# Up units of 256, 256 and 128 slots in one PSUM bank each, four units deep

## The chip, the cores and the metric

One core of one Trainium2 chip runs the kernel. The metric is the device time of one execution in microseconds; smaller is better. Engines: PE multiplies matrices (PEld is its weight loading), DVE and ACT work elementwise, POOL issues the indirect DMAs here, SP the plain ones.

## The reference, cut to what matters

A layer norm and a selective scan come first; the change does not touch them. Then comes a mixture of experts over T = 2048 tokens of width 128, with 8 experts of hidden width 512, the two best experts per token and 640 slots per expert:

```python
pre = jnp.einsum('ech,edh->ecd', expert_inputs, ff_pre_act_weight)
gate = jnp.einsum('ech,edh->ecd', expert_inputs, gate_weight)
expert_out = jnp.einsum('ecd,ehd->ech', pre * jax.nn.silu(gate), ff_post_act_weight)
updates = eo_flat[dispatch] * kept_w.astype(x.dtype)[:, None]
out = jnp.zeros((T, DMODEL), x.dtype).at[st].add(updates)
```

`expert_inputs` is 8 x 640 x 128, the rows of the tokens chosen for each expert.

## The kernel before

Everything is float32. The expert stage begins at about 204 us of a span of 352 us. Experts 0 to 7 are worked off one after another, each over 640 slots (`CAP`), as five tiles of 128 slots (`NQ` = 5) on the slot side and four chunks of 128 on the hidden side (`FC` = 4). The queues of all engines are written out by hand and meet in semaphores. For expert e:

- POOL (`gather`, L1213) fetches the 640 rows with five indirect DMAs, by the index list `gid` that DVE writes (L804), and later adds the 640 results to `out` with five more (L1230). Its order is: gathers of expert e + 2, then scatters of expert e. Ahead of the first scatter of an expert it waits until all earlier scatters have landed (`s_scattered`). Experts 6 and 7 have no gathers ahead of their scatters.
- PE turns the rows (`turn`, L1506) for the next expert; ACT and DVE split them into a high and a low f32r part (L1056, L1058, L821).
- `up` (L1517): a *unit* is one chunk of 128 hidden rows by one half of the slots (`HALF` = 320). A unit needs the gate product and the value product, each of them three f32r matmuls of 128x128 weights by 320 columns (`three`, L1510: high by high, high by low, low by high). There are 8 units, so 48 matmuls. The gate goes to PSUM bank 2 or 3, the value to bank 0 or 1, by the unit's parity. PE may start the gate of unit g when the silu of unit g - 2 has read its bank (`s_silu`), and its value when DVE has multiplied unit g - 2 (`s_hidden`).
- ACT (`gates`, L1060) applies silu to a unit's gate (L1067) into one of two `sg` buffers, and between the first five units scales one tile of the previous expert's result each (`weigh`, L1083), which that expert's scatter waits for. In the last two units it also copies the next expert's up weights (L1050).
- DVE (`expert`, L830) first computes the scatter ids and weights of the expert (`scatter_rows`, L812 to L815), for which it waits until the scatters of expert e - 2 have landed. Then for each unit it multiplies value by silu into `hT` (L841) and builds two of the 16 one-hot blocks of expert e + 2 (L787). Then come `columns`, `tokens_low`, `weights_low`, and `gather_rows(e + 2)`, which turns the table into `gid`.
- PE then runs `down` (L1537, 40 matmul instructions, two per f32 product) in three parts, with `turn` for expert e + 1 after the first part and `table(e + 2)` (L1491) ahead of the last. `table(e + 2)` needs the one-hots, and `gid` of expert e + 2 needs the table.
- SP (L422 to L426) reloads the weight buffers when `s_in_low` and `s_down` say that they are free.

So the path from one expert to POOL's next burst of gathers is: scatters of e - 2 landed, DVE `scatter_rows(e)`, first product, PE's remaining up units, part of `down` and `turn`, `table(e + 2)`, `gid`, gathers of e + 2.

`last_expert` (L1559) interleaves the up units of expert 7 with its down tiles, which go to PSUM banks of their own. `keep_clock` runs matmuls on zeros ahead of the stage.

Of the kernel before, what the change touches and what calls it, by code (L numbers as in the profile page):

```python
# [27 lines left out]
ALU = mybir.AluOpType  # L28
# [6 lines left out]
NT = T // P  # L35
# [23 lines left out]
HALF = CAP // 2  # L59
# [45 lines left out]
def build(nc, x, wx, wdt, vectors, dskip, w1, wg, w2, consts, jbits, out, rows):  # L105
    with ExitStack() as ctx:
# [116 lines left out]
        sg = later(2, HALF)  # L223
# [209 lines left out]
        def _(dve):  # L433
# [396 lines left out]
            def expert(e, b, more, split=True, last=False):  # L830
# [4 lines left out]
                for un in range(2 * FC):  # L835
                    half, f = un // FC, un % FC
                    dve.wait_ge(s_silu, e * (2 * FC) + (un + 1))
                    if un == 0:
                        if above_zero(e - 1):
                            dve.wait_ge(s_down, e - 1)  # L840
                    v.tensor_tensor(hT[:, b, f, half * HALF:(half + 1) * HALF], psum[:, un % 2, 0:HALF],  # L841
                                    sg[:, un % 2, :], ALU.mult).then_inc(s_hidden, 1)
                    if more:
                        for j in range(un * NT // (2 * FC), (un + 1) * NT // (2 * FC)):
                            one_hot(e + 2, j)
# [40 lines left out]
        def _(act):  # L886
# [165 lines left out]
            def spread_tokens(e, b):  # L1052
                if above_zero((e - 1) * 2 * FC):
                    act.wait_ge(s_up, (e - 1) * 2 * FC)
# [5 lines left out]
            def gates(e, b, i, split, first=False, last=False):  # L1060

                for un in range(2 * FC):
                    g = e * (2 * FC) + un
                    act.wait_ge(s_up, g + 1)
                    if above_zero(g - 1):
                        act.wait_ge(s_hidden, g - 1)
                    a.activation(sg[:, un % 2, :], psum[:, 2 + un % 2, 0:HALF], ACT.Silu).then_inc(s_silu, 1)  # L1067
                    if not first and un < NQ:
                        weigh(e - 1, 1 - b, un)
                    if last and un == 2 * FC - 2:  # L1070
                        weigh_last(e, b, range(2))
                    if split and un >= 2 * FC - 2:
                        if un == 2 * FC - 2:
                            act.wait_ge(s_in_weights[1 - b], 32 * (i + b) + 32)
                        weights_high(e + 1, 1 - b, un - 2 * FC + 2)
# [174 lines left out]
        def _(pe):  # L1250
# [266 lines left out]
            def up(e, b, units):  # L1517
                if 0 in units:
                    pe.wait_ge(s_in_low, 2 * e + 2)
                for un in units:  # L1520
                    half, f = un // FC, un % FC
                    g = e * (2 * FC) + un
                    pe.wait_ge(s_xe_low, 2 * e + 1 + half)
                    if above_zero(g - 1):
                        pe.wait_ge(s_silu, g - 1)
                    cs = slice(half * HALF, (half + 1) * HALF)
                    three(psum[:, 2 + un % 2, 0:HALF], f, b, 0, cs)
                    if above_zero(g - 1):
                        pe.wait_ge(s_hidden, g - 1)
# [89 lines left out]
```

## Time and profile before

| | us |
|---|---|
| median of 3 runs | 355.86 |
| lowest and highest | 352.87, 357.71 |
| the profiled execution | 354.3 |
| its span | 352.3 |
| PE busy (share of span) | 272.9 (77%) |
| DVE busy | 255.8 (73%) |
| POOL busy | 216.3 (61%) |
| PE weight loads busy | 195.2 (55%) |
| ACT busy | 131.8 (37%) |

The shares are means over the whole span; in the first half DVE's scan sets the pace, in the expert stage the shares are others. The rows shown further down are from the stage from 204 us on, apart from one. In a timeline row the first number is the start in us from the span's start, the second the length of the instruction, or of the merged run of equal ones. Matmuls overlap, so the length of one is more than the distance to the next; the distance from one start to the next (the pitch) is the rate. "[0.30 <-issue]" means that the engine was idle 0.30 us before, and what ended that.

### The profile page before, as it was taken

The page shows a single profiled execution, that of the slowest core. Times are in us where ns is not written, and L with a number is a line of the kernel's source. Part 1 is how long each engine was busy: PE and PEld are TensorE (multiplying, and loading weights), DVE is VectorE, ACT ScalarE, POOL GpSimd, SP SyncE. Part 2 cuts the span into 40 slices and gives each one's busy share as a digit, 9 for nine tenths or more (in the row PEclk, how much of TensorE's full clock was granted, in tenths as well). Part 3 has the DMA queues.
Part 4 walks back from the last instruction along what each step waited for, and adds up shares of the span by engine and source line. Part 5 has one row for each costly group of instructions (what it writes and reads, how often), then busy time and mean ns, then how long its engine had stood idle before and what let it go on. Part 6 is the DMA issues. An engine that isn't in the chain of part 4 may idle for free.

```text
span 352.3 us, 5061 instructions
## 1 busy us (share of the span) xinstructions
PE 272.9 (77%) x1432; PEld 195.2 (55%) x1432; DVE 255.8 (73%) x599; ACT 131.8 (37%) x270; POOL 216.3 (61%) x152
## 2 busy tenths in 40 slices
PE   5979997589688959866970868995979798978830
PEld 3345443145354425433460557994979798878730
DVE  2788599999999999999988855683757576533400
ACT  3374793415254244433102004361535244434410
POOL 2555637698656747565715055178888787876863
PEclk9895899769899989998995799999898989989995
DMA  7013004239200000000011012056253535423322
GB/s 217 0 40 82 0 4 116 60 84 243 100 31 0 0 30 30 0 30 30 0 55 64 3 32 46 7 130 130 43 134 40 134 33 136 63 47 37 33 22 22
DMA packets 20755, 20.30 MB, mean 58 GB/s; under 512 B 2624, under 2 KB 14848, under 8 KB 20736
## 3 DMA queue, kind: packets, MB, share of 16 engines
q1 hardware_dynamic: 13184, 14.63, 14.7%
q0 software_dynamic: 7040, 5.25, 11.5%
q10 hardware_dynamic: 512, 0.19, 0.3%
q8 instruction: 9, 0.15, 0.2%
q14 instruction: 10, 0.08, 0.1%
HBM read 10.82 MB, written 5.05 MB: 45 GB/s over the span
## 4 chain that ended last, share of the span: by engine, by line
DVE 25%; issue 21%; PE 20%; POOL 18%; DMA 9%; ACT 4%; POOLq 1%; DVEq 1%; ACTq 0%
POOL out L1230 10%; DMA out<-ring,sid 7%; DVE psum L525 6%; DVE ring L535 5%; POOL ring L1158 4%; PE psum L1513 3%; PE psum L1515 2%; PE psum L1514 2%; PE psum L1326 1%; PE psum L1298 1%; POOL parts L1143 1%; PE psum L1364 1%; PE psum L1534 1%; DMA small<-in_small 1%; DVE sm L558 1%
## 5 line engine op out<-in xcount | busy, mean ns | idle before, releaser
L1158 POOL TENSOR_TENSOR ring<-ring,cbc 128x1024 f32<-128x1024 f32 x31 | 73.2, 2363 | 44.6 <-DVE ring L535 44.2
L1230 POOL DMA_INDIRECT out<-ring,sid x40 | 64.0, 1601 | 16.8 <-issue 10.7
L1326 PE MATMUL psum<-stack,sel_r 128*128 (+1 forms) x120 | 51.6, 526 | 24.5 <-DVE ring L535 22.5
L1364 PE MATMUL psum<-ring,cst 128*128 128x512 f32 x128 | 67.2, 654 | 0.9 <-POOL ring L1158 0.9
L1213 POOL DMA_INDIRECT ring<-rows,gid x40 | 38.9, 971 | 36.4 <-issue 23.3
L535 DVE TENSOR_TENSOR_SCAN ring<-ring,psum 128x1024 f32<-128x1024 f32 x25 | 57.1, 2285 | 1.6
L1513 PE MATMUL psum<-stack 128*128 128x320 f32 x128 | 43.9, 343 | 15.0 <-DVE ring L841 14.4
L962 ACT ACTIVATE ring<-psum,nega 128x510 f32<-128x510 f32 x64 | 40.6, 681 | 38.2 <-PE psum L1326 35.4
L1326 PEld LDWEIGHTS psum<-stack,sel_r 128*128 128x128 f32 x120 | 22.1, 201 | 51.9 <-DVE ring L535 24.2
L1067 ACT ACTIVATE ring<-psum 128x320 f32<-128x320 f32 x64 | 27.9, 438 | 61.0 <-PE psum L1515 60.6
L841 DVE TENSOR_TENSOR ring<-psum,ring 128x320 f32<-128x320 f32 x64 | 31.2, 491 | 18.9 <-ACT ring L1067 17.6
L1515 PE MATMUL psum<-stack 128*128 128x320 f32 x128 | 42.3, 331 | 0.0
L1514 PE MATMUL psum<-stack 128*128 128x320 f32 x128 | 42.3, 330 | 0.0
L1534 PE MATMUL psum<-w_s,ring 128*128 128x128 f32 x320 | 40.0, 277 | 1.1 <-DVE ring L841 1.1
L1364 PEld LDWEIGHTS psum<-ring,cst 128*128 128x128 f32 x128 | 25.9, 209 | 24.1 <-issue 20.2
L1534 PEld LDWEIGHTS psum<-w_s,ring 128*128 128x128 f32 x320 | 37.7, 192 | 1.5 <-DVE ring L841 1.3
L1513 PEld LDWEIGHTS psum<-stack 128*128 128x128 f32 x128 | 26.6, 207 | 17.0 <-DVE ring L841 16.0
L525 DVE TENSOR_TENSOR psum<-psum,bbc 128x512 f32<-128x512 f32 x50 | 31.7, 680 | 0.0
L1298 PE MATMUL psum<-zero 128*128 128x256 bf16 x182 | 26.3, 307 | 6.0 <-DMA cst<-in_consts 3.5
L1298 PEld LDWEIGHTS psum<-zero 128*128 128x128 bf16 x182 | 19.6, 110 | 12.6 <-issue 5.2
L787 DVE TENSOR_SCALAR ring<-iota_b,r 128x128 bf16<-128x128 bf16 x128 | 26.5, 269 | 0.0
L1514 PEld LDWEIGHTS psum<-stack 128*128 128x128 f32 x128 | 26.5, 207 | 0.0
(181 smaller groups left out, 352.8 us busy)
## 6 DMA issues: line engine op xcount, KB each, us to landing
stack<-parts SPq DMA_DIRECT2D x16, 256.0 KB, 3.8
win_s<-in_wg SPq DMA_DIRECT2D x8, 256.0 KB, 3.6
win_s<-in_w SPq DMA_DIRECT2D x8, 256.0 KB, 4.3
w_s<-in_w SPq DMA_DIRECT2D x8, 256.0 KB, 2.9
xt<-in_x SPq DMA_DIRECT2D x4, 256.0 KB, 4.5
out<-xt SPq DMA_DIRECT2D x4, 256.0 KB, 2.3
rows<-xn SPq DMA_DIRECT2D x4, 256.0 KB, 2.3
ring<-rows,gid POOLq DMA_INDIRECT x40, 3.1
```

The source lines that it names most:

```text
L525: v.tensor_tensor(dst, src, bbc[:, bass.ts(c, CH)], ALU.mult).then_inc(s_input, 1)
L535: v.tensor_tensor_scan(hh[:, s].rearrange("p a b -> p (a b)"), da[:, s].rearrange("p a b -> p (a b)"), inputs.rearrange("p a b -> p (a b)" ...
L962: a.activation(dst[:, :, 1:], src[:, :, 1:], ACT.Exp, scale=nega[:, g:g + 1]).then_inc(s_decay, 1)
L1158: g.tensor_tensor(hc[:, s], hh[:, s], cb, ALU.mult).then_inc(s_product, 1)
L1230: g.indirect_dma_start(out=out, out_offset=bass.IndirectOffsetOnAxis(ap=sid[:, b, q:q + 1], axis=0), in_=ye[:, b, q, :], in_offset=None, c ...
L1298: mm(bank(junk, 2 * D), z[:, 0:P], z, start=True, stop=True)
L1326: ins = mm(bank(to), sel, stack[:, half, kind, bass.ts(c, CH)], start=True, stop=True)
L1364: ins = mm(bank(YB), wred[:, o:o + D], hc[:, s, k, :], start=(grp == 0), stop=(grp == NG - 1))
L1513: mm(out_, win_p[:, b, 0, k, fs], xe_p[:, b, 0, cs], start=True, stop=False)
L1514: mm(out_, win_p[:, b, 0, k, fs], xe_p[:, b, 1, cs], start=False, stop=False)
L1515: return mm(out_, win_p[:, b, 1, k, fs], xe_p[:, b, 0, cs], start=False, stop=True)
L1534: ins = mm(place, hT[:, b, f, q * P:(q + 1) * P], w2_s[:, b, f, :], start=(f == 0), stop=(f == FC - 1))
```

## The change

The slots of a chunk are cut in pieces of 256, 256 and 128 (`PIECES`) in place of two halves of 320, so an expert has `UNITS` = 12 units in place of 8. A unit's gate takes columns 0 to 255 and its value columns 256 to 511 of one PSUM bank, and four banks and four `sg` buffers are used in turn (`DEPTH` = 4). Both products of unit g now wait for one thing, the product of unit g - 4 on DVE (`s_hidden`). The silu of a unit waits for the same. The one-hots of an expert are spread over 12 units. The down tiles wait for the pieces that they read. The weight copies of ACT stay in the last two units of an expert. `weigh` stays in the first five.

```diff
--- before.py
+++ after.py
@@ -56,7 +56,10 @@
 CAP = 640
 NQ = CAP // P
 QA = 3
-HALF = CAP // 2
+
+PIECES = ((0, 256), (256, 512), (512, CAP))
+UNITS = len(PIECES) * FC
+DEPTH = 4
 EPS_LN = 1e-05
 EPS_W = 1.1920929e-07
 NROUND = 8
@@ -220,7 +223,7 @@
         stack_flat = stack[:].rearrange("p h k t -> p (h k t)")
         win_p = stack_flat[:, 0:8 * DFF].rearrange("p (b i k f) -> p b i k f", b=2, i=2, k=2)
         xe_p = stack_flat[:, 8 * DFF:8 * DFF + 4 * CAP].rearrange("p (b i n) -> p b i n", b=2, i=2)
-        sg = later(2, HALF)
+        sg = later(DEPTH, 256)
         hT = later(2, FC, CAP)
         ye = later(2, NQ, D)
         zero = sb("zero", [P, D])
@@ -832,16 +835,16 @@
                 scatter_rows(e, b)
                 if more:
                     dve.wait_ge(s_table, e + 2)
-                for un in range(2 * FC):
-                    half, f = un // FC, un % FC
-                    dve.wait_ge(s_silu, e * (2 * FC) + (un + 1))
+                for un in range(UNITS):
+                    (lo, hi), f = PIECES[un // FC], un % FC
+                    dve.wait_ge(s_silu, e * UNITS + (un + 1))
                     if un == 0:
                         if above_zero(e - 1):
                             dve.wait_ge(s_down, e - 1)
-                    v.tensor_tensor(hT[:, b, f, half * HALF:(half + 1) * HALF], psum[:, un % 2, 0:HALF],
-                                    sg[:, un % 2, :], ALU.mult).then_inc(s_hidden, 1)
+                    v.tensor_tensor(hT[:, b, f, lo:hi], psum[:, un % DEPTH, 256:256 + hi - lo],
+                                    sg[:, un % DEPTH, 0:hi - lo], ALU.mult).then_inc(s_hidden, 1)
                     if more:
-                        for j in range(un * NT // (2 * FC), (un + 1) * NT // (2 * FC)):
+                        for j in range(un * NT // UNITS, (un + 1) * NT // UNITS):
                             one_hot(e + 2, j)
                 if more:
                     columns(e + 2)
@@ -1050,8 +1053,8 @@
                 a.activation(win_p[:, b, 0, k], win_s[:, b, k], ACT.Copy).then_inc(s_in_high, 1)
 
             def spread_tokens(e, b):
-                if above_zero((e - 1) * 2 * FC):
-                    act.wait_ge(s_up, (e - 1) * 2 * FC)
+                if above_zero((e - 1) * UNITS):
+                    act.wait_ge(s_up, (e - 1) * UNITS)
                 act.wait_ge(s_rows_turned, 2 * e + 1)
                 a.activation(xe_p[:, b, 0, 0:QA * P], bank(4, QA * P), ACT.Copy).then_inc(s_xe, 1)
                 act.wait_ge(s_rows_turned, 2 * e + 2)
@@ -1059,20 +1062,21 @@
 
             def gates(e, b, i, split, first=False, last=False):
 
-                for un in range(2 * FC):
-                    g = e * (2 * FC) + un
+                for un in range(UNITS):
+                    lo, hi = PIECES[un // FC]
+                    g = e * UNITS + un
                     act.wait_ge(s_up, g + 1)
-                    if above_zero(g - 1):
-                        act.wait_ge(s_hidden, g - 1)
-                    a.activation(sg[:, un % 2, :], psum[:, 2 + un % 2, 0:HALF], ACT.Silu).then_inc(s_silu, 1)
+                    if above_zero(g - (DEPTH - 1)):
+                        act.wait_ge(s_hidden, g - (DEPTH - 1))
+                    a.activation(sg[:, un % DEPTH, 0:hi - lo], psum[:, un % DEPTH, 0:hi - lo], ACT.Silu).then_inc(s_silu, 1)
                     if not first and un < NQ:
                         weigh(e - 1, 1 - b, un)
-                    if last and un == 2 * FC - 2:
+                    if last and un == UNITS - 2:
                         weigh_last(e, b, range(2))
-                    if split and un >= 2 * FC - 2:
-                        if un == 2 * FC - 2:
+                    if split and un >= UNITS - 2:
+                        if un == UNITS - 2:
                             act.wait_ge(s_in_weights[1 - b], 32 * (i + b) + 32)
-                        weights_high(e + 1, 1 - b, un - 2 * FC + 2)
+                        weights_high(e + 1, 1 - b, un - UNITS + 2)
 
             def weigh(e, b, q):
                 if q == 0:
@@ -1518,16 +1522,13 @@
                 if 0 in units:
                     pe.wait_ge(s_in_low, 2 * e + 2)
                 for un in units:
-                    half, f = un // FC, un % FC
-                    g = e * (2 * FC) + un
-                    pe.wait_ge(s_xe_low, 2 * e + 1 + half)
-                    if above_zero(g - 1):
-                        pe.wait_ge(s_silu, g - 1)
-                    cs = slice(half * HALF, (half + 1) * HALF)
-                    three(psum[:, 2 + un % 2, 0:HALF], f, b, 0, cs)
-                    if above_zero(g - 1):
-                        pe.wait_ge(s_hidden, g - 1)
-                    three(psum[:, un % 2, 0:HALF], f, b, 1, cs).then_inc(s_up, 1)
+                    (lo, hi), f = PIECES[un // FC], un % FC
+                    g = e * UNITS + un
+                    pe.wait_ge(s_xe_low, 2 * e + 1 + (un >= FC))
+                    if above_zero(g - (DEPTH - 1)):
+                        pe.wait_ge(s_hidden, g - (DEPTH - 1))
+                    three(psum[:, un % DEPTH, 0:hi - lo], f, b, 0, slice(lo, hi))
+                    three(psum[:, un % DEPTH, 256:256 + hi - lo], f, b, 1, slice(lo, hi)).then_inc(s_up, 1)
 
             def down_tile(b, q, place):
                 for f in range(FC):
@@ -1540,14 +1541,14 @@
                     if above_zero(NQ * e):
                         pe.wait_ge(s_weighed, NQ * e)
 
-                pe.wait_ge(s_hidden, e * 2 * FC + (FC if tiles[-1] < 2 else 2 * FC))
+                pe.wait_ge(s_hidden, e * UNITS + FC * (tiles[-1] // 2 + 1))
                 for q in tiles:
                     ins = down_tile(b, q, psum[:, 5 + q // 4, (q % 4) * P:(q % 4 + 1) * P])
                 return ins
 
             def expert(i, b, more=True):
                 e = 2 * i + b
-                up(e, b, range(2 * FC))
+                up(e, b, range(UNITS))
                 down(e, b, i, range(0, 2))
                 turn(e + 1, 1 - b, i + b)
                 down(e, b, i, range(2, 4))
@@ -1561,12 +1562,12 @@
                 up(e, b, range(FC + 2))
                 pe.wait_ge(s_out_weights[b], 16 * (E // 2))
                 pe.wait_ge(s_weighed, NQ * e)
-                pe.wait_ge(s_hidden, e * 2 * FC + FC)
+                pe.wait_ge(s_hidden, e * UNITS + FC)
                 for q in range(2):
                     down_tile(b, q, bank(LAST_BANK[q], P)).then_inc(s_down_tile, 1)
-                up(e, b, range(FC + 2, 2 * FC))
-                pe.wait_ge(s_hidden, (e + 1) * 2 * FC)
+                up(e, b, range(FC + 2, UNITS))
                 for q in range(2, NQ):
+                    pe.wait_ge(s_hidden, e * UNITS + FC * (q // 2 + 1))
                     down_tile(b, q, bank(LAST_BANK[q], P)).then_inc(s_down_tile, 1)
 
             keep_clock(WARM["slots"], 3)
```

## Rows read from the trace of the kernel before

**Rows 1.** Windows of all engines: stretch, length, busy us (count) per engine, PEclk.

```profile
213.90:221.70 7.80, 7.25 (x49) 6.93 (x48) 5.81 (x24) 4.63 (x9) 2.66 (x3) 1.00 0.17 35
...
227.80:323.70 95.90, 83.14 (x645) 81.64 (x644) 57.31 (x197) 39.38 (x103) 77.52 (x60) 0.93 0.45 85
```

**Rows 2.** Timeline, POOL: start us, us taken, instruction, [idle before <-releaser].

```profile
227.85 0.95 POOL L1213 DMA_INDIRECT ring<-rows,gid  x1 [10.68 <-DVE gid L804]
...
243.49 1.02 POOL L1213 DMA_INDIRECT ring<-rows,gid  x1 [0.30 <-issue]
...
259.69 1.02 POOL L1213 DMA_INDIRECT ring<-rows,gid  x1 [0.30 <-issue]
...
292.39 1.02 POOL L1213 DMA_INDIRECT ring<-rows,gid  x1 [0.63 <-issue]
...
308.21 1.02 POOL L1213 DMA_INDIRECT ring<-rows,gid  x1 [0.30 <-ACT ring L1083]
...
326.25 1.56 POOL L1230 DMA_INDIRECT out<-ring,sid  x1 [2.57 <-DVE kw L815]
```

**Rows 3.** Timeline, DVE: where each `gid` is written, experts 0, 1, 2, 4, 5.

```profile
226.85 0.17 DVE L804 TENSOR_SCALAR gid<-token 128x5 int32<-128x5 f32 x1
...
239.65 0.17 DVE L804 TENSOR_SCALAR gid<-token 128x5 int32<-128x5 f32 x1
...
258.29 0.17 DVE L804 TENSOR_SCALAR gid<-token 128x5 int32<-128x5 f32 x1
...
291.26 0.17 DVE L804 TENSOR_SCALAR gid<-token 128x5 int32<-128x5 f32 x1
...
304.94 0.17 DVE L804 TENSOR_SCALAR gid<-token 128x5 int32<-128x5 f32 x1
```

**Rows 4.** Timeline, PE and ACT, up units of expert 0.

```profile
213.72 0.38 PE L1513 MATMUL psum<-stack 128*128 128x320 f32 x1
...
214.39 1.28 ACT L1067 ACT_TABLE_LOAD   x1
...
216.27 0.39 PE L1513 MATMUL psum<-stack 128*128 128x320 f32 x1 [0.55 <-ACT ring L1067]
...
217.02 0.31 PE L1514 MATMUL psum<-stack 128*128 128x320 f32 x1
...
221.72 1.95 PE L1534 MATMUL psum<-w_s,ring 128*128 128x128 f32 x16
```

**Rows 5.** Timeline, PE and DVE, up units of expert 3.

```profile
258.45 0.39 PE L1513 MATMUL psum<-stack 128*128 128x320 f32 x1
...
261.91 0.17 DVE L812 SCALAR_TENSOR_TENSOR tk<-tab,cst 128x5 f32<-128x5 f32 x1 [3.45 <-DMA out<-ring,sid]
...
262.37 0.49 DVE L841 TENSOR_TENSOR ring<-psum,ring 128x320 f32<-128x320 f32 x1
...
262.91 0.42 PE L1513 MATMUL psum<-stack 128*128 128x320 f32 x1 [2.02 <-DVE ring L841]
...
263.10 0.48 DVE L841 TENSOR_TENSOR ring<-psum,ring 128x320 f32<-128x320 f32 x1
...
264.03 0.47 PE L1513 MATMUL psum<-stack 128*128 128x320 f32 x1
...
269.38 1.95 PE L1534 MATMUL psum<-w_s,ring 128*128 128x128 f32 x16
```

**Rows 6.** Timeline, PE: narrow matmuls with four-byte weights.

```profile
101.94 0.95 PE L1383 MATMUL psum<-small,x2T 128*128 128x8 f32 x8
...
223.50 0.71 PE L1506 MATMUL psum<-cst,ring 128*128 128x128 f32 x5
...
224.05 1.95 PE L1534 MATMUL psum<-w_s,ring 128*128 128x128 f32 x16
```

**Rows 7.** Groups of instructions by line and form, ACT, 200 us to the end.

```profile
L1067 ACT ACTIVATE ring<-psum 128x320 f32<-128x320 f32 x64 | 27.9, 438 | 61.0 <-PE psum L1515 60.6
...
L1083 ACT ACTIVATE ring<-psum,kw 128x128 f32<-128x128 f32 x35 | 12.7, 362 | 0.0
```

## The prediction

> **What bounds the kernel now.** I read the expert stage (213 us to the end), since the change touches nothing ahead of it, and start with POOL, which issues all gathers and scatters. The window of 227.8 to 323.7 us holds 60 POOL instructions with 77.52 us of busy time [rows 1]. Each follows its predecessor by at least 0.30 us, so they fill 77.5 + 60 x 0.30 = 95.5 of 95.9 us. POOL's timeline agrees: the idle time before the six five-gather bursts is 10.68 us once, then 0.30 four times and 0.63 before the fifth [rows 2]. From 227.85 us POOL is the bound. After the last gathers it waits 2.57 us [rows 2]: `s_scattered` guards the first scatter of an expert, and the same landing released DVE; the gap ahead of expert 7's scatters is alike. The up stage does not set these.
>
> What can delay POOL is the index list `gid`. The first burst in the loop starts 227.85 - 226.85 = 1.00 us after `gid` starts on DVE [rows 2, 3]. Taking 1.00 us for all, the margins between "list usable" and "POOL free" are:
> - gid(3), made by expert 1: 243.49 - 240.65 = 2.8 us.
> - gid(4) by expert 2: 259.69 - 259.29 = 0.40. gid(5), made by expert 3, repeats this within 0.01.
> - gid(6) by expert 4: late. POOL idled 0.63 instead of 0.30, so 0.33 us late.
> - gid(7) by expert 5: 308.21 - 305.94 = 2.3 [rows 2, 3].
>
> So two loops are almost balanced: POOL's 16.0 us per expert, and a chain "last scatter of e-2 lands, DVE starts expert e, PE finishes up(e), down, table(e+2), gid(e+2)". In expert 3 that chain reads: PE starts at 258.45, runs dry, DVE is released by the landing at 261.91, multiplies at 262.37, PE resumes at 262.91 after 2.02 us of idle and ends the up units at 269.38 [rows 5]. It also restarts at the lower clock: a matmul then takes 0.47 instead of 0.31 us [rows 4, 5], and 320 columns at 1.2 GHz are 0.267 us against a pitch of 0.147. That is the 1.2 GHz level, granted after idling; expert 0, which waits only 0.55 us, keeps a granted clock of 1.00 [rows 1, 4].
>
> **What changes, and its price.**
>
> 1. *PE pitch.* At 320 columns the pitch is (221.72 - 217.02) / 32 = 0.1469 us [rows 4], or 1.10 times 320 columns at 2.4 GHz. For 256 columns the same rate gives 0.117 us. For 128 columns it would give 0.059, but another limit shows: eight matmuls that move only 8 columns, with 128x128 four-byte weights, take 0.95 us with the drain of the last, so 0.10 to 0.12 each, and five 128-column transposes take (224.05 - 223.50) / 5 = 0.110 [rows 6]. Eight columns of data cannot cost that; loading the weights does. The f32 down products, two passes each, take (223.50 - 221.72) / 16 = 0.111 a pass [rows 4, 6]. I take 0.111. Bounds: 0.059 (the load hides) and 0.222 (as dear as the two passes of a plain f32 product, twice 0.111); nearest in weights and width are the transposes, so 0.111.
>    Before, one expert has 48 matmuls: 48 x 0.1469 = 7.05 us. After, 72: 48 x 0.117 + 24 x 0.111 = 5.62 + 2.66 = 8.28 us. **PE gets 1.2 us more work per expert**, all from re-loading weights for a third, narrow piece.
>    The rows show a floor near 0.11 us with such weights. The Trainium skill (TensorE: Matmul & The Clock Gate, Back-to-back issue gap) gives about 81 ns per matmul at N=128 in a stream of loads and matmuls; by it the 24 would cost 1.94 and the expert 7.6 us. Its section on LDWEIGHTS gives P/1.2, or 107 ns, and there this trace agrees.
>
> 2. *Expert 0, nothing to wait for.* Before, PE stops 0.55 us after two units, because the first silu sits behind a 1.28 us table load [rows 4]. Four units deep it does not: four units last 4 x 6 x 0.117 = 2.81, until 213.80 + 2.81 = 216.6, and the first product is done at about 216.6 as well. Before: 221.72 - 213.72 = 8.00. After: 8.28 + 0.08 (first matmul) + 0.05 for that product = 8.4. The path goes on through down and table to gid(2), which opens POOL's unbroken run: **+0.4 us**. It is not hidden. Bounds: -0.8 (pitch 0.059) and +3.1 (0.222).
>
> 3. *Expert 1.* No landing holds it. 8.4 against 7.1, 1.3 more; the 2.8 us margin covers it: 0. With the dear pitch, 3.9 more: 1.1 late.
>
> 4. *Experts 2 to 4, released by a landing.* The deeper buffer lets PE do 4 of 12 units ahead, 24 matmuls of 256 columns. Before it was not 2 but 2.5 units: the gate half of the third unit waits on `s_silu` alone, and 15 matmuls were done: 0.08 + 15 x 0.147 = 2.3 us from 258.45, and PE ran dry at 262.91 - 2.02 = 260.89, the drain of the last included. Work left after the release: before, 33 x 0.1469 = 4.85 us; after, 24 x 0.117 + 24 x 0.111 = 5.47. The first product of 256 columns is about 0.07 us shorter than the 0.49 for 320. Net **+0.56 us of chain**, if the clock does the same. The gate waiting for `s_hidden` now, not `s_silu`, is queued before down, turn and table, and is part of this. Against the margins: expert 2, 0.56 - 0.40 = 0.16 late. Expert 3 is released by a scatter issued before that slip, so it meets a POOL that is 0.16 later and has 0.41 + 0.16: 0. Expert 4: its margin is spent, all 0.56 is lost. Expert 5 has 2.3. **Sum +0.7 us.**
>    The clock can give something back. In expert 3 PE would run dry at 258.53 + 2.81 + 0.15 (drain) = 261.5 and idle 1.4 us, not 2.0. If that keeps the higher clock, the cost of the slow restart (269.38 - 262.91 = 6.47 us for 4.85 us of work [rows 5], so 1.6) vanishes, the chain is short and expert 4's 0.33 returns: the sum of this item is then -0.2. In expert 2 the landing comes later against PE's start, and its idle stays long. I take **+0.4**, nearer the first, as the idle shrinks by only 0.6 us.
>
> 5. *DVE and ACT.* DVE steps from one product over two one-hots to the next in 263.10 - 262.37 = 0.73 us [rows 5]; with 1.33 one-hots per unit and 64 fewer columns it needs about 0.55, and PE offers a unit every 0.70 (256) or 0.67 (128): hidden. Twelve units instead of eight cost DVE about 0.3 us per expert. ACT: a 320-column silu takes 438 ns and a weigh 362 [rows 7]; even unoverlapped, about 0.75 us for a unit with a weigh is near PE's 0.70, and four of the five weighs now come before the release, while scatters need them later (first scatter of the run behind five gathers). Hidden; if that cover went, 0.2 us.
>
> 6. *Weights, w2 and tail.* SP's loads wait for `s_in_low` and `s_down`, which shift with the chain and have many us in hand. In experts 6 and 7 POOL waits for landings; PE's last down tile can slip by several us. `weigh_last` is now behind unit 10 of 12: 0.
>
> Sum: 0.4 + 0.4 = **+0.8 us**. The profiled execution took 354.3 us (span 352.3), so 355.1 by that one; the median of the runs is 355.86, which is 1.6 above it, so **356.7 us** as a median. The forecast is no change that can be told: a measurement of this kernel tells about 2% apart (the three runs spread over 1.4%).
>
> **Rivals.**
> - *Dear narrow pieces (slower).* An f32r matmul of 128 columns costs 0.222, not 0.111. Then +3.1 at expert 0, +1.1 at expert 1, and in experts 2 to 5 the work after the release (2.81 + 5.33 = 8.1 us) uses every margin: about 0.2, 1.0, 0.5 and 0.6. Sum +6.5, 362.4 us. It decides from about 0.15 us per narrow matmul. For: plain f32 needs two passes of 0.111. Against: at 320 columns f32r needs one pass. 0.15.
> - *The lower clock lasts longer.* If the narrow matmuls keep PE slow twice as long after each restart, each released chain grows 1.6 more: 0.4 + (0.16 + 1.6) + 0 + (0.56 + 1.6) = +4.3, 360.2 us. Against: PE idles less than before. 0.10.
> - *Faster.* The chain of waits of the page leads through DVE's product and PE's restart in experts 2 to 5. Were this the bound, the shorter idle would pay. But POOL's run has no holes of more than 0.3 us to give. With narrow matmuls at 0.059, the clock kept, and POOL's bursts at their shortest (5 x 0.95 + 5 x 1.56 = 12.55 us, six times 75.3 against 77.5) it is -0.8 - 0.3 - 2.2 = -3.3, 352.6 us. 0.12.
> - The forecast, 354.8 to 358.5: 0.63.
>
> **Chances and range.** The dear pitch (0.15) stays partly out, the others are in: 352.5 to 361.0. Above 2% (363.0) lies about half of the dear case and a little of the slow-clock case together with the spread of runs: 0.11. Below -2% (348.7) nothing in the sums reaches, only what I have not seen: 0.06. Same 0.83.
>
> **What would show it.** Pitch of the 128-column matmuls near 0.111 and 256 near 0.117; PE in an expert without a wait 8.4 us; POOL still unbroken from its first loop burst (now near 228.3) to 324; PE's restart wait in expert 3 about 1.4 us; five-gather bursts with idle 0.30 except one or two of 0.4 to 1.2. Wrong if POOL's run shows holes over 1 us (the chain has become the bound), if the narrow pitch is off 0.111 by half, or if POOL's instructions themselves change length.

## The result: 0.8% slower, with two holes in POOL's run

| | before | after |
|---|---|---|
| median, us | 354.19 (20 runs) | 357.58 (20 runs) |
| lowest, highest, us | 352.38, 357.71 | 354.32, 362.92 |
| profiled execution, us | 354.3 | 357.1 |
| its span, us | 352.3 | 355.2 |

The ratio of after to before is 1.0082, with a 95% interval of 1.0053 to 1.011: about 2.9 us slower, and no change by the 2% bound. It is taken from fast runs alone (slow ones are over 1.5% above the fastest of their kernel, five of the 20 after), while the medians in the table are over all 20.

First the page of the kernel after, busy time of each engine. Before had 1432 matmuls and now there are 1624, 64 x 3 more.

```profile
PE 279.4 (79%) x1624; PEld 204.3 (58%) x1624; DVE 260.1 (73%) x631; ACT 136.4 (38%) x302; POOL 216.0 (61%) x152
```

A window of the kernel after, all engines (length, then busy us and count of each, PEclk, DMA share, GB/s). This one is POOL's run over the six bursts of the loop.

```profile
226.90:326.80 99.90, 89.13 (x791) 88.44 (x791) 60.37 (x221) 43.44 (x128) 77.21 (x60) 0.95 0.44 82
```

POOL's 60 instructions are as busy as before, 77.21 us where they were 77.52 [rows 1], but from the first burst's start to the end of the last scatter (326.67) they take 99.67 us, where before they took 95.83. The timeline of POOL in the kernel after shows where: the first burst of gathers, the last scatter of expert 0, the first gathers of the third and of the fifth burst, then the first scatter of expert 6.

```profile
227.00 0.94 POOL L1217 DMA_INDIRECT ring<-rows,gid  x1 [11.36 <-DVE gid L807]
...
240.91 1.55 POOL L1234 DMA_INDIRECT out<-ring,sid  x1 [0.30 <-issue]
...
260.82 1.01 POOL L1217 DMA_INDIRECT ring<-rows,gid  x1 [2.61 <-DVE gid L807]
...
294.79 1.01 POOL L1217 DMA_INDIRECT ring<-rows,gid  x1 [2.47 <-DVE gid L807]
...
329.16 1.56 POOL L1234 DMA_INDIRECT out<-ring,sid  x1 [2.49 <-ACT ring L1087]
```

Against [rows 2], the idle time ahead of the third burst grew from 0.30 to 2.61 us and ahead of the fifth from 0.63 to 2.47: **4.15 us of new holes**, both put down to `gid`. The second, fourth and sixth burst start 0.30 to 0.31 us after the instruction ahead of them, as before.

The whole, in the two profiles: the front of the kernel ended 1.5 us earlier in the one after (expert 0's up units start at 212.22, before at 213.72 [rows 4]). The change doesn't touch it, and over the kernels of this study that point varies from 210.5 to 213.7. From there to the first burst 14.78 us instead of 14.13, +0.65. From the first burst to the last scatter's start (348.27, before 345.37) 121.27 instead of 117.52, +3.75. From there to the end 6.93 in both. So -1.5 + 0.65 + 3.75 = +2.9, the difference of the spans. The stretch that the change touches cost 4.4 us in this pair; the ratio says about 3.

### The loads that meet the scatter

The timelines of DVE in the kernel after: where the landing of expert 0's (2's) last scatter releases expert 2 (4), and the `gid` that comes out at the end of that expert.

```profile
246.26 0.17 DVE L815 SCALAR_TENSOR_TENSOR tk<-tab,cst 128x5 f32<-128x5 f32 x1 [5.99 <-DMA out<-ring,sid]
...
259.69 0.17 DVE L807 TENSOR_SCALAR gid<-token 128x5 int32<-128x5 f32 x1
...
280.24 0.17 DVE L815 SCALAR_TENSOR_TENSOR tk<-tab,cst 128x5 f32<-128x5 f32 x1 [6.44 <-DMA out<-ring,sid]
```

Expert 0's last scatter starts on POOL at 240.91, so its landing took 246.26 - 240.91 = **5.35 us**. The same two rows of the kernel before, its POOL and its DVE timeline:

```profile
241.63 1.56 POOL L1230 DMA_INDIRECT out<-ring,sid  x1 [0.30 <-issue]
```

```profile
245.46 0.17 DVE L812 SCALAR_TENSOR_TENSOR tk<-tab,cst 128x5 f32<-128x5 f32 x1 [5.64 <-DMA out<-ring,sid]
```

245.46 - 241.63 = **3.83 us**. For expert 2's last scatter it is 5.20 after (275.04 to 280.24), 4.75 before (273.68 to 278.43). These times hold POOL's own part, which took 2.06 us instead of 1.56 in that scatter of before; counted from the end of POOL's part, the landing is 3.80 against 2.27 us behind expert 0, and 3.64 against 2.69 behind expert 2. Expert 1's took 4.44 us before, and after had landed when DVE came to it. Those of experts 3 to 5 take 3.3 to 3.6 us in both kernels. The queue of SP shows what else is on the way at that time. After, the issues of the reloads of `w2` for expert 3 and of `wg` and `w1` for expert 4, of 256 KB each:

```profile
240.49 0.33 SPq L429 DMA_DIRECT2D w_s<-in_w  x1
241.39 0.33 SPq L426 DMA_DIRECT2D win_s<-in_wg  x1
241.82 0.38 SPq L427 DMA_DIRECT2D win_s<-in_w  x1
```

Before:

```profile
240.03 0.33 SPq L426 DMA_DIRECT2D w_s<-in_w  x1
240.94 0.33 SPq L423 DMA_DIRECT2D win_s<-in_wg  x1
241.37 0.38 SPq L424 DMA_DIRECT2D win_s<-in_w  x1
```

These issues stand 0.5 us later against the span, but the last scatter stands 0.7 us earlier. Before, the scatter starts 1.6 us after the first of them and behind all three; after, it starts 0.4 us after the first and ahead of two. When the third load lands is in the DMA views, before and after (the last number is us from issue to landing):

```profile
win_s<-in_w SPq DMA_DIRECT2D x1, 256.0 KB, 3.8
```

```profile
win_s<-in_w SPq DMA_DIRECT2D x1, 256.0 KB, 4.1
```

That is 245.2 us before and 245.9 after, and DVE is released at 245.46 and 246.26, 0.3 us behind it in both. The traces of the kernels below repeat this: in all 11 cases with loads of full size in which DVE waited and the third of them (in experiment 5 the last) was issued at most 1.6 us after the start of the scatter, the release came within 0.45 us of this load's landing; in the three cases in which it was issued 2.4 to 2.7 us after (before, experts 1 to 3) the scatter landed ahead of it. Read so, the 1.52 us are the third load landing 0.75 us later and the scatter starting 0.72 us earlier. That the loads lengthen the landing is a reading so far; the first, second and fifth experiment test it.

### The profile page after: what moved, and what is told of

Read it like the earlier page. It is cut to its first block, busy times and chain, and to the rows that moved or that the text cites. A ratio compares the mean times of both kernels' runs of the same rounds, so it can differ in the third digit from the quotient of the medians.

```text
span 355.2 us, 5593 instructions
## 1 busy us (share of the span) xinstructions
PE 279.4 (79%) x1624; PEld 204.3 (58%) x1624; DVE 260.1 (73%) x631; ACT 136.4 (38%) x302; POOL 216.0 (61%) x152
## 4 chain that ended last, share of the span: by engine, by line
PE 27%; DVE 24%; POOL 17%; issue 17%; DMA 7%; ACT 4%; POOLq 1%; DVEq 1%; ACTq 1%
POOL out L1234 8%; DVE ring L538 6%; DMA out<-ring,sid 5%; POOL ring L1162 4%; DVE psum L528 4%; PE psum L1535 4%; PE psum L1517 3%; POOL ring L1217 3%; PE psum L1519 3%; PE psum L1518 3%; PE psum L1368 3%; PE psum L1330 2%; PE psum L1284 1%; PE psum L1274 1%; POOL parts L1147 1%
## 5 line engine op out<-in xcount | busy, mean ns | idle before, releaser
L1330 PE MATMUL psum<-stack,sel_r 128*128 (+1 forms) x120 | 50.7, 521 | 25.1 <-DVE ring L538 23.1
L1368 PE MATMUL psum<-ring,cst 128*128 128x512 f32 x128 | 66.3, 647 | 0.9 <-POOL ring L1162 0.9
L1517 PE MATMUL psum<-stack 128*128 128x256 f32 (+1 forms) x192 | 56.7, 295 | 12.0 <-DVE ring L844 12.0
L1071 ACT ACTIVATE ring<-psum 128x256 f32<-128x256 f32 (+1 forms) x96 | 33.2, 348 | 59.9 <-PE psum L1519 58.1
L1518 PE MATMUL psum<-stack 128*128 128x256 f32 (+1 forms) x192 | 55.8, 291 | 0.0
L1519 PE MATMUL psum<-stack 128*128 128x256 f32 (+1 forms) x192 | 55.7, 290 | 0.0
L844 DVE TENSOR_TENSOR ring<-psum,ring 128x256 f32<-128x256 f32 (+1 forms) x96 | 35.8, 378 | 19.9 <-ACT ring L1071 17.4
L1517 PEld LDWEIGHTS psum<-stack 128*128 128x128 f32 x192 | 38.9, 203 | 12.9 <-DVE ring L844 8.7
L1518 PEld LDWEIGHTS psum<-stack 128*128 128x128 f32 x192 | 39.0, 203 | 0.0
L1519 PEld LDWEIGHTS psum<-stack 128*128 128x128 f32 x192 | 38.8, 202 | 0.0
L790 DVE TENSOR_SCALAR ring<-iota_b,r 128x128 bf16<-128x128 bf16 x128 | 28.7, 264 | 0.0
```

The costliest lines, as they stand in the source:

```text
L1330: ins = mm(bank(to), sel, stack[:, half, kind, bass.ts(c, CH)], start=True, stop=True)
L1368: ins = mm(bank(YB), wred[:, o:o + D], hc[:, s, k, :], start=(grp == 0), stop=(grp == NG - 1))
L1517: mm(out_, win_p[:, b, 0, k, fs], xe_p[:, b, 0, cs], start=True, stop=False)
L1518: mm(out_, win_p[:, b, 0, k, fs], xe_p[:, b, 1, cs], start=False, stop=False)
L1519: return mm(out_, win_p[:, b, 1, k, fs], xe_p[:, b, 0, cs], start=False, stop=True)
```

## The experiments

The theory: the extra pitch gives the chain about 0.6 us, and the rest of the holes is the landing, stretched by SP's reloads. The rivals: the narrow matmuls or the new order on PE, DVE and ACT cost the time directly (then quiet DMA queues don't help), or POOL isn't the bound. All ratios are to the kernel before on the same chip, with their 95% intervals. "The chain" is the time from the release of DVE by the landing to the `gid` at the end of that expert.

### 1. The reloads wait for the scatters

In the kernel after, SP waits for the landing of the expert's scatters before it reloads `w2` for every second expert:

```diff
                     sp.wait_ge(s_down, 2 * i + (b + 1))
+                    if b:
+                        sp.wait_ge(s_scattered, 32 * NQ * i + 16 * NQ)
                     nc.sync.dma_start(w2_s[:, b, :, :], ...
```

> The changed kernel, but SP holds the reload of the odd expert's w2 (and what is queued behind it) until the scatters of the expert before have landed. In the changed kernel the last scatter of expert 0 starts at 240.91 us and DVE is released at 246.26, 5.35 us later; before it was 241.63 to 245.46, 3.83. The 256 KB reloads start at 240.49, 241.39 and 241.82. Theory L (the lateness of the gathers of experts 4 and 6, two POOL holes of 2.61 and 2.47 us, comes in good part from the scatter's landing being slowed by the reloads): landing back to about 3.4 us, the first hole falls from 2.6 to about 0.7, the second to about 0.8 to 1.0, the time to about 1.000 of the kernel before. Rival C (the longer PE work after the release and its lower clock alone make the holes): both holes stay above 2 us, time stays at 1.008.

Measured: 359.4 us, 1.018 (1.0114 to 1.0247), in four runs. Expert 0's last landing fell to 3.44 us, but the wait only moved the loads. SP's queue in this kernel:

```profile
245.56 0.33 SPq L431 DMA_DIRECT2D w_s<-in_w  x1
...
257.95 0.33 SPq L431 DMA_DIRECT2D w_s<-in_w  x1
258.54 0.33 SPq L426 DMA_DIRECT2D win_s<-in_wg  x1
258.97 0.39 SPq L427 DMA_DIRECT2D win_s<-in_w  x1
```

The second three now surround the next expert's last scatter (start 258.31), and the DVE timeline shows it landing after 5.13 us:

```profile
263.44 0.17 DVE L817 SCALAR_TENSOR_TENSOR tk<-tab,cst 128x5 f32<-128x5 f32 x1 [5.76 <-DMA out<-ring,sid]
```

The holes come back one burst later, 2.99 us at 278.74 and 2.15 at 312.43. The first has the long landing behind it, so the landing followed the loads, which speaks for the collision. The second has not: expert 3's last scatter (start 292.95) also had three loads around it, issued from 291.98 to 293.00, and landed after 3.80 us. In both the chain was longer as well, 14.18 and 14.56 us instead of 13.43: PE restarted at 1.2 GHz and took 7.93 and 8.32 us to the end of the up units, where after took 7.10. As a repair it failed, and the forecast of its time with it. Expert 0's up stage ran at the lower clock in this profile too (9.64 us, where after took 8.60), so its whole time is not a measure of the wait alone.

### 2. Next to no reloads

The kernel after with 32 of 512 columns of `wg` and `w1`, and 32 columns of one chunk of `w2`, reloaded for experts 2 to 7; the rest of these weights is left out, so those experts compute with old ones. Everything else is unchanged.

```diff
-nc.sync.dma_start(win_s[:, b, 0, :], wg[2 * i + (2 + b)])
+nc.sync.dma_start(win_s[:, b, 0, 0:32], wg[2 * i + (2 + b)][:, 0:32])
...
-nc.sync.dma_start(w2_s[:, b, :, :], w2[2 * i + (2 + b)])
+nc.sync.dma_start(w2_s[:, b, 0, 0:32], w2[2 * i + (2 + b)][:, 0, 0:32])
```

> The changed kernel with the weight reloads of experts 2 to 7 cut to 32 of 512 columns (w1, wg) and one chunk's 32 columns (w2), so those experts compute with wrong weights: the same queues and semaphores, almost no bytes. Theory L: landing near 3.3 us everywhere, holes as with the reloads held back, 0.5 to 1.0 us each, time 1.000 to 1.002 of before. Rival C: holes above 2 us, 1.008.

Measured: 353.14 us, 0.9983 (0.9945 to 1.0022). POOL's timeline, the last scatter of expert 0 and the two bursts that had the holes:

```profile
241.31 1.55 POOL L1234 DMA_INDIRECT out<-ring,sid  x1 [0.30 <-issue]
...
259.31 1.02 POOL L1217 DMA_INDIRECT ring<-rows,gid  x1 [0.31 <-issue]
...
291.63 1.01 POOL L1217 DMA_INDIRECT ring<-rows,gid  x1 [0.30 <-issue]
```

DVE's timeline, the release:

```profile
244.71 0.17 DVE L815 SCALAR_TENSOR_TENSOR tk<-tab,cst 128x5 f32<-128x5 f32 x1 [4.02 <-DMA out<-ring,sid]
```

The landing is 244.71 - 241.31 = 3.40 us, all six are between 3.2 and 3.8, there is no hole where 0.5 to 1.0 us were expected, and the time is that of the kernel before. All 72 matmuls per expert are still there. The rival that the new units cost the time directly falls: without the reloads their extra work lies beside POOL, apart from expert 0. A second thing helped: in experts 2 and 4 PE idled only 2.01 and 0.66 us and restarted at 2.4 GHz, and the chain took 11.94 us in both instead of 13.43. The landing alone would have been just enough: with after's chain, `gid` would have been usable 0.04 us ahead of POOL in both.

### 3 and 4. The chain without the landing, in both kernels

DVE's `scatter_rows`, which waits for the landing, moves behind the expert's products and columns, so that PE and `gid` no longer hang on it (last expert excepted; the `gather_rows` behind it waits for its results):

```diff
-                scatter_rows(e, b)
+                if last:
+                    scatter_rows(e, b)
...
                 if not last:
+                    scatter_rows(e, b)
+                if not last:
                     tokens_low(e + 1, 1 - b)
...
+                if not last:
+                    dve.wait_ge(s_scatter_ids, 2 * e + 2)
                 if more:
```

On the kernel after:

> The changed kernel, but DVE computes an expert's scatter ids and weights behind its unit loop and columns instead of ahead (except for the last expert), so its first product no longer waits for the landing of the scatters two experts back. The chain from landing to gather list is gone. Both theories: PE never idles long in experts 2 to 6, no hole above 0.3 us before the gathers of experts 3 to 7, POOL unbroken. If only the chain cost time, what stays is expert 0's longer up stage, +0.4 to +0.7 us: ratio 1.001 to 1.002 of before. If the extra PE work (1.2 to 1.5 us per expert) costs time anywhere else, it stays above 1.005.

On the kernel before:

> The kernel before with the same move of the scatter ids. If POOL was the bound from its first burst on, as the prediction reads it, removing PE's waits of 2 to 4.7 us in each of experts 2 to 6 gives only the 0.33 us of expert 4: ratio 0.998 to 1.000. If the chain of waits through DVE's product and PE's restart was the bound, as the page's chain would have it, it gives 1 us or more per expert, 0.985 to 0.99.

Measured: 352.29 us, 0.999 (0.9952 to 1.0028), for the changed units; 352.96 us, 0.9991 (0.9946 to 1.0035), for the old ones. POOL's timeline with the changed units, the two bursts:

```profile
258.58 1.01 POOL L1222 DMA_INDIRECT ring<-rows,gid  x1 [0.30 <-ACT ring L1092]
...
290.50 1.04 POOL L1222 DMA_INDIRECT ring<-rows,gid  x1 [0.31 <-issue]
```

With the landing off the chain the new units cost nothing against the old, and in the kernel before the same step gains nothing that can be told: there the chain was just covered by POOL, which confirms POOL as its bound. PE's stalls in the up stages of experts 2 to 6 are gone in both kernels; what PE still waits for in these experts are gathered rows, in `turn`, 2.2 us at most each, and they leave no hole in POOL's run. (In the second kernel's profile expert 0 ran at the lower clock, 9.8 us, so a small gain may be hidden in it.)

### 5. More loads, old units

The kernel before with two more loads of 256 KB into a scratch tile, right ahead of each reload of `wg` for an even expert:

```diff
                     sp.wait_ge(s_in_low, 4 * i + (2 * b + 2))
+                    if b == 0:
+                        sp.wait_ge(s_extra, 32 * i + 16)
+                        for k in range(2):
+                            nc.sync.dma_start(scratch[:, k, :], w1[2 * i + 2 + k]).then_inc(s_extra, 16)
```

> The kernel before, with two further 256 KB loads into an unused tile put in SP's queue ahead of each reload of an even expert's gate weights, so with about twice the bytes in flight when the last scatters of experts 0 and 2 land. Nothing of the up units is changed. Theory L: these landings grow from 3.83 and 4.75 us to 5.5 or more, and since the margins of the gathers of experts 4 and 6 are +0.40 and -0.33 us, holes of 1 to 2.5 us appear ahead of both; ratio 1.005 to 1.012. Rival C (holes come from PE's longer work): the landings may move but no hole over 1 us, ratio 0.999 to 1.003.

Measured: 355.88 us, 1.0086 (1.0053 to 1.0118), the slowdown of the change with none of its units. POOL's timeline, the last scatter of expert 0 and the two bursts:

```profile
240.14 1.55 POOL L1238 DMA_INDIRECT out<-ring,sid  x1 [0.30 <-issue]
...
260.57 1.02 POOL L1221 DMA_INDIRECT ring<-rows,gid  x1 [3.13 <-DVE gid L812]
...
294.26 1.02 POOL L1221 DMA_INDIRECT ring<-rows,gid  x1 [2.20 <-DVE gid L812]
```

DVE's:

```profile
246.19 0.17 DVE L820 SCALAR_TENSOR_TENSOR tk<-tab,cst 128x5 f32<-128x5 f32 x1 [7.85 <-DMA out<-ring,sid]
```

The landing takes 246.19 - 240.14 = 6.05 us. Expert 2's last one takes 4.79, as before's 4.75, so the second hole isn't explained by its own landing alone. The trace has the rest. From the end of POOL's part this landing is 3.23 us against 2.69, +0.54. The chain, with the old units, is 13.60 us against 12.83, +0.77, since PE idled 5.96 us ahead of it instead of 2.28 and took 7.26 us from the restart to the end of the up units instead of 6.49. POOL's own instructions took 0.26 us less. With the 0.33 us of lateness of before that is 1.90 us, the hole less the usual 0.30. So a long landing costs twice where PE's longer idle also lengthens the stretch at 1.2 GHz.

### 6 and 7. What the parts of the change cost

New pieces with the old buffers (two banks, two units deep, the gate waiting on `s_silu`):

```diff
-DEPTH = 4
+DEPTH = 2
...
-three(psum[:, un % DEPTH, 0:hi - lo], f, b, 0, slice(lo, hi))
+three(psum[:, 2 + un % DEPTH, 0:hi - lo], f, b, 0, slice(lo, hi))
```

> The pieces alone: 256, 256 and 128 slots as in the changed kernel, but gate and value in two banks, two units deep, with the waits of the kernel before. PE is 2.5 units ahead at a release (15 matmuls of 256), so 33 x 0.120 + 24 x 0.111 = 6.6 us remain, against 5.6 in the changed kernel: chain 1.1 us longer, holes ahead of the gathers of experts 4 and 6 near 3.4 us if the landings are alike; expert 0 waits for the silu table again, 9.8 against 8.6 us. Ratio about 1.015 to 1.02. If depth is worth nothing, it stays at 1.008.

Measured: 363.25 us, 1.0297 (1.025 to 1.0344). PE's timeline in expert 0:

```profile
213.45 0.36 PE L1517 MATMUL psum<-stack 128*128 128x256 f32 x1 [0.83 <-ACT ring L1071]
```

and POOL's two holes:

```profile
262.72 1.01 POOL L1217 DMA_INDIRECT ring<-rows,gid  x1 [4.42 <-DVE gid L807]
...
298.03 1.01 POOL L1217 DMA_INDIRECT ring<-rows,gid  x1 [3.81 <-DVE gid L807]
```

So the pieces alone cost 3%, more than the 1.5 to 2 expected, and the deeper buffer, with the one bank per unit that comes with it, gives back 2 of them: two short units cover less of what the units wait for. Expert 0 takes 10.03 us and expert 1 9.06, where four deep they take 8.60 and 8.46, and from the restart after expert 2's release to the end of its up units it is 9.43 us, where four deep it is 7.10. A part of that is the clock, which stood at 1.2 GHz for longer after the restart than in the kernel after; no run takes the two apart.

Nearly equal pieces, with four units deep as in the change (the down tiles wait for the pieces that they now read):

```diff
-PIECES = ((0, 256), (256, 512), (512, CAP))
+PIECES = ((0, 216), (216, 432), (432, CAP))
```

> The changed kernel with pieces of 216, 216 and 208 slots. If the pitch has a floor of 0.111 us from the weight load, all 72 matmuls take 0.111: expert 1's up stage 8.0 to 8.1 us against 8.46; at 1.10 columns per 2.4 GHz cycle they would take 0.099, 7.1 us. The chain then shortens by 0.2 us (48 matmuls left), the holes stay near 2 us where the landings are slow. Ratio 1.005 to 1.009; by the pitch without a floor 1.002.

Measured: 355.74 us, 1.0083 (1.0044 to 1.0121). PE's timeline in expert 1, its first matmul and the first of its down products:

```profile
224.33 0.35 PE L1517 MATMUL psum<-stack 128*128 128x216 f32 x1
...
232.44 0.40 PE L1535 MATMUL psum<-w_s,ring 128*128 128x128 f32 x2
```

72 matmuls in 8.11 us: every one at 0.111 to 0.113, whether it moves 216 or 208 columns, as the 128-column ones did. The floor is not the data's. That it is the four-byte weights' and not that of any matmul shows in the table products of the kernel after, 16 matmuls with 128x128 weights of two bytes, and what follows them:

```profile
224.98 0.56 PE L1495 MATMUL psum<-rq,ring 128*128 128x25 bf16 x16
225.39 1.14 PE L1535 MATMUL psum<-w_s,ring 128*128 128x128 f32 x8
```

They take (225.39 - 224.98) / 16 = 0.026 us each. Spreading the columns evenly saves 0.35 us of 8.46, and the holes remain (2.75 us at 259.62 and at 293.61; landings 5.11 and 4.64 us). The chain of expert 2, expected 0.2 us shorter, was 0.8 longer in this profile, 14.21 us (244.28 to 258.49), as PE restarted at 1.2 GHz (granted clock 0.50 in the first us, where the kernel after had 0.86). So what a shorter chain is worth while the landing is long, this run doesn't show.

### 8. A version ahead of both

The kernel before with the late `scatter_rows` of experiment 4, and one silu on a tile of 128x1 ahead of expert 0, so that the table load doesn't sit on expert 0's path:

```diff
+            a.activation(early[:], bdt_s, ACT.Silu)
             spread_tokens(0, 0)
```

> The kernel before with the late scatter ids and one silu on a 128x1 tile ahead of expert 0, so that the 1.28 us table load is done while ACT is idle. PE's wait of 0.55 us in expert 0 goes: that stage 7.1 to 7.5 us instead of 8.0, POOL's first burst 0.55 us earlier, and POOL unbroken behind it. Ratio 0.997 to 0.999. Should POOL not be the bound, nothing changes against the version with late ids alone, 0.999.

Measured: 351.71 us, 0.9958 (0.9923 to 0.9994). PE's timeline, the up units of expert 0:

```profile
212.10 0.38 PE L1519 MATMUL psum<-stack 128*128 128x320 f32 x1
...
219.27 0.38 PE L1540 MATMUL psum<-w_s,ring 128*128 128x128 f32 x2
```

7.17 us, where before took 8.00 [rows 4]; and no hole in POOL's run. That run is no shorter, 95.99 us from the first burst to the end of the last scatter against 95.83: the gain lies ahead of it. The whole interval is below 1, if by little: this one is faster than before, and 1.2% faster than after (ratio of the ratios, 0.9958 / 1.0082 = 0.988).

## Why the prediction was nearly right, step by step

The forecast was 356.7 us in 352.5 to 361.0, no change that can be told; it came as 357.58. The sign, the place and the bound were right. The size was not: the sum said +0.8 us, the ratio says +2.9, and most of the closeness is luck in the base, as the 355.86 used for it was 1.7 above the 354.19 that more runs gave. And what the prediction itself named as a sign of being wrong, holes over 1 us in POOL's run, came.

**What POOL's run is.** Right: it bounds before, and the holes appear in the bursts behind experts 2 and 4, with nothing behind 1, 3 and 5. Expert 3 was costed at 0 and is 0.

**Pitch.** The timeline of PE in the kernel after, expert 0:

```profile
212.22 0.36 PE L1517 MATMUL psum<-stack 128*128 128x256 f32 x1
...
215.24 0.36 PE L1517 MATMUL psum<-stack 128*128 128x256 f32 x1
...
218.36 0.27 PE L1519 MATMUL psum<-stack 128*128 128x128 f32 x1
...
220.70 0.28 PE L1519 MATMUL psum<-stack 128*128 128x128 f32 x1
220.82 0.44 PE L1535 MATMUL psum<-w_s,ring 128*128 128x128 f32 x2
```

The 128-column pitch is (220.70 - 218.36) / 21 = 0.1114 us: forecast 0.111, right, and the rival of dear narrow pieces (0.222) is out. The 256-column one is 0.120 (18 in 216.03 to 218.19), forecast 0.117; scaling by columns from 320 was 0.003 low. An expert without a wait takes 8.46 us (expert 1, 226.28 to 234.74), forecast 8.4, with before's at 7.2. The Trainium skill (TensorE: Matmul & The Clock Gate, Back-to-back issue gap) would have had 81 ns for the narrow ones; the measured 0.1114 decides, and the P/1.2 of its section on LDWEIGHTS, 107 ns, is the figure that the trace agrees with, for weights of four bytes (those of two bytes in experiment 7 took 26 ns with their matmul).

**Expert 0.** Forecast +0.4 us; 8.60 instead of 8.00, and +0.65 up to the first burst. The stall behind the table load did shrink, from 0.55 to 0.08 us; the difference is the pitch, 48 x 0.003 = 0.15 us, and small things. Right in kind, 0.2 short.

**Chain from release to `gid`.** Forecast +0.56 us. Measured 246.26 to 259.69, or 13.43, against 245.46 to 258.29 [rows 3], or 12.83: **+0.60**. Expert 4 gives +0.59. The steps that made this up (four units ahead, 24 + 24 matmuls left, the slow restart) were each right: after the restart at 247.29 the up units end at 254.39, 7.10 us, forecast 5.47 of work and 1.6 of the lower clock. The windows of PE alone in the kernel after show that clock (length, busy, PEclk, DMA share, GB/s):

```profile
240.00:247.00 7.00, 3.32 (x29) 1.00 0.67 150
247.00:249.00 2.00, 1.71 (x10) 0.76 0.26 66
249.00:251.00 2.00, 2.00 (x12) 0.50 0.22 33
251.00:253.00 2.00, 2.00 (x18) 0.89 0.36 33
```

1.2 GHz after an idle of 3.97 us, and 2.4 again within 6 us, as before: the rival that it lasts longer with narrow matmuls is out in this trace (restart to end 7.10 us, 1.55 over its work; before 6.48, 1.63 over). In some of the other kernels it lasted longer, behind other idle times.

**The step that failed: how late the release is.** The prediction costed step 6, SP's reloads, at 0, since their waits "have many us in hand", and took the landing of the last scatter as given. It looked at when the loads are needed, not at what else is on the way when they run. In the kernel after the landing, counted from the end of POOL's part, is 1.53 us longer behind expert 0 and 0.95 behind expert 2. How late `gid` then is for POOL, in us, from both traces:

| | third burst | fifth burst |
|---|---|---|
| margin (-) or lateness (+) before | -0.27 | +0.33 |
| chain from release to `gid` | +0.60 | +0.59 |
| landing of the last scatter, from the end of POOL's part | +1.53 | +0.95 |
| POOL reaches the burst sooner after that point | +0.45 | +0.30 |
| sum, and idle time less 0.30 | 2.31 | 2.17 |
| forecast of this lateness | 0.16 | 0.89 |

The first line differs from the prediction's 0.40, which took 1.00 us from `gid` to the gather, read at the first burst; where a gather inside POOL's run waited for `gid` it started 1.13 us behind it (292.39 - 291.26 [rows 2, 3], 260.82 - 259.69). The fourth line is a second thing taken as fixed. The margins were read against before's POOL, whose scatters were partly stretched: the one at 257.47 took 1.92 us, those at 288.07 and 290.09 1.72 and 1.67, where most take 1.55. After, POOL needs 0.45 and 0.30 us less between the same points, so it is free earlier and meets `gid` later. "POOL's instructions change length" stood among what would make the prediction wrong; 4.15 us of holes less 0.31 us of shorter instructions is what the run grew by.

**PE's idle in expert 3.** Forecast 1.4 us instead of 2.02, with a chance that the clock stays high. Measured 0: the hole ahead of the third burst put expert 3 later against the scatter that releases it, PE never stopped, and `gid` came at 273.63, 2.3 us before POOL wanted it. It gave the loop nothing, since there was slack there already. In experts 2 and 4 PE still stops, 3.97 and 4.36 us, as the timeline says:

```profile
247.29 0.38 PE L1517 MATMUL psum<-stack 128*128 128x256 f32 x1 [3.97 <-DVE ring L844]
...
281.26 0.39 PE L1517 MATMUL psum<-stack 128*128 128x256 f32 x1 [4.36 <-DVE ring L844]
```

**DVE and ACT.** Hidden, as forecast. The groups of ACT by form in the kernel after, from 200 us on:

```profile
L1071 ACT ACTIVATE ring<-psum 128x256 f32<-128x256 f32 x64 | 24.4, 384 | 51.4 <-PE psum L1519 49.5
L1087 ACT ACTIVATE ring<-psum,kw 128x128 f32<-128x128 f32 x35 | 12.6, 361 | 0.0
L1071 ACT ACTIVATE ring<-psum 128x128 f32<-128x128 f32 x32 | 8.8, 276 | 8.6 <-PE psum L1519 8.6
```

A silu and a weigh are 0.384 + 0.361 = 0.745 us beside PE's unit of 0.72; the sum was 0.75, and 58.1 of the 60.0 us of ACT's idle time before the silus are spent on PE.

**What stays open.** Experiments 2 and 5 show that the amount of reloading decides whether there is a landing of 3.4 or of 5 to 6 us behind expert 0, and experiment 1 that the long landing moved with the loads once, and once did not (3.80 us). That the release comes with the landing of the third load is a coincidence in 11 cases; how the two streams share the way, in the DMA engines or behind them, no run here shows. The landings are from one profile of each kernel. What lengthens the stretch at 1.2 GHz after a restart is open. Nor is it shown which stretches POOL's instructions (below).

## What to carry to other kernels

When two loops are balanced within half a microsecond, an edit that only adds a little work on an idle engine moves every later issue, and a transfer that was free can land on one that is waited for: before costing a load at nothing, look at which completions are awaited while it runs. Take a margin against the shortest the other loop can do, not against what one profile shows. And splitting f32r matmuls below about 216 columns saves nothing per matmul, since the load of 128x128 four-byte weights costs 0.111 us each for 128 to 216 columns. A deeper buffer without narrower pieces might be better than either kernel, but no run here has one.

## What the runs showed of the hardware

- An indirect scatter (128 rows, 64 KB) took 3.2 to 3.8 us from its start on POOL to the release of DVE with next to no other loads, and 3.8 to 6.05 us where it met 256 KB loads on SP's queue, by how they fell.
- POOL's own part of a scatter took 1.55 us in most cases and 1.7 to 2.06 in some. The stretched ones often coincide with DVE's subtraction over 128x512 f32: in the kernel after, one of 1.89 us at 272.85 with two such from 272.01 on; before, the 2.06 at 273.68 with two from 273.02. A coincidence in several rows; no run took it apart.
- Expert 0's up stage ran at 1.2 GHz for 12 to 22 of its matmuls in two of the kernels (experiments 1 and 4), behind the same instructions as in the others, and at 2.4 GHz throughout in before and after. It costs 1 to 1.8 us on the path, as much as half of the effect studied, and what decides it is open.
